# The head of an int4 SwiGLU + S4 kernel: token blocks transposed operand by operand, sums in place, buffers moved, all engines reordered until unit 2

## What is computed

```
xn = layernorm(x)
out = x + s4(xn) + ffn(xn)

# ffn: int4 weights, groups of 64 with scale and zero
Wg, Wu, Wd = dequantize(gate_Wq, ...), dequantize(up_Wq, ...), dequantize(down_Wq, ...)
h = silu(xn @ Wg.T) * (xn @ Wu.T)      # 2048 x 2752
ffn = h @ Wd.T                         # 2048 x 1024

# s4: a kernel of 1024 taps from 64 complex states (Cauchy sums at the roots of unity, inverse FFT),
# then a causal convolution of each row with it, plus D * xn
```

## Time and profile before

| | us |
|---|---|
| median of 3 runs | 1380.62 |
| lowest, highest | 1374.71, 1381.23 |
| the profiled execution | 1377.99 |
| its span in the trace | 1376.2 |

### The profile page before, as it was taken

How to read it: one execution, slowest core, us unless ns; L and a number is a source line. 1 busy time by engine, 2 the same in 40 slices (tenths; PEclk the granted TensorE clock), 3 DMA queues, 4 the chain that set the end, 5 groups by cost and what they waited for, 6 DMA issues and landing times.

```text
span 1376.2 us, 16940 instructions
## 1 busy us (share of the span) xinstructions
PE 1313.8 (95%) x6302; PEld 625.4 (45%) x6302; DVE 917.0 (67%) x1008; ACT 461.8 (34%) x815; POOL 665.4 (48%) x484
## 2 busy tenths in 40 slices
PE   3688999999999999999999999899999999999998
PEld 2454444444444444444444444344444444444444
DVE  7965798989989889997797977434434423241432
ACT  5744444555455454544454544310000000000000
POOL 6862776878878787875686877520000000000000
PEclk8799999999999999999999999999999999999999
DMA  9111554454646454544455455999373344336331
GB/s 315 34 47 39 156 159 153 141 181 146 187 131 187 138 179 126 171 152 123 151 153 163 127 157 161 366 395 324 102 235 123 100 156 166 115 100 222 100 100 61
DMA packets 165168, 218.08 MB, mean 158 GB/s; under 512 B 42205, under 2 KB 122719, under 8 KB 163167
## 3 DMA queue, kind: packets, MB, share of 16 engines
q1 hardware_dynamic: 163646, 200.69, 46.7%
q10 hardware_dynamic: 1440, 16.32, 2.9%
HBM read 139.64 MB, written 77.34 MB: 158 GB/s over the span
## 4 chain that ended last, share of the span: by engine, by line
PE 76%; DVE 5%; issue 1%; ACT 1%; POOL 1%; DMA 0%; SPq 0%; ACTq 0%; DVEq 0%
PE px L1382 24%; PE px L1469 17%; PE pz L1382 11%; PE pz L1469 8%; PE py L1382 6%; PE pv L1496 6%; PE py L1469 4%; DVE wf L1554 1%; DVE wf L1551 1%; DVE wf L1555 0%; DMA w_d<-ds 0%; POOL ds L703 0%; DVE hf L1682 0%; POOL hs L713 0%; DVE hf L1685 0%
## 5 line engine op out<-in xcount | busy, mean ns | idle before, releaser
L1382 PE MATMUL px<-xo,wo 128*128 128x512 f16 x2016 | 467.1, 385 | 13.3 <-ACT u L1006 9.5
L1382 PEld LDWEIGHTS px<-xo,wo 128*128 128x128 f16 x2016 | 199.4, 99 | 256.7 <-issue 19.4
L694 POOL TENSOR_TENSOR wo<-wf,wo 128x512 f16<-128x512 f32 x147 | 233.7, 1600 | 69.1 <-ACT wo L952 69.1
L713 POOL TENSOR_TENSOR hs<-hf,hs 128x512 f16<-128x512 f32 x154 | 204.3, 1332 | 99.5 <-ACT hs L987 97.2
L1469 PE MATMUL px<-wd,hr 128*128 128x512 f16 x1056 | 232.3, 379 | 0.0
L1382 PE MATMUL pz<-xo,wo 128*128 128x512 f16 x1008 | 231.3, 379 | 0.1
L1469 PEld LDWEIGHTS px<-wd,hr 128*128 128x128 f16 x1056 | 102.2, 98 | 118.8
L1382 PEld LDWEIGHTS pz<-xo,wo 128*128 128x128 f16 x1008 | 98.6, 98 | 118.6 <-issue 0.8
L952 ACT ACTIVATE wo<-wf 128x512 f16<-128x512 f32 x147 | 91.5, 623 | 89.0 <-DVE wf L1555 81.2
L1554 DVE TENSOR_TENSOR wf<-wf,sz 128x1024 f32<-128x1024 int32 x63 | 118.4, 1879 | 2.2
L1469 PE MATMUL pz<-wd,hr 128*128 128x512 f16 x528 | 116.6, 379 | 0.0
(11 more groups left out here) (230 smaller groups left out, 1387.4 us busy)
## 6 DMA issues: line engine op xcount, KB each, us to landing
h_d<-hs SPq DMA_DIRECT2D x154, 256.0 KB, 2.4
hr<-h_d SPq DMA_DIRECT2D x56, 704.0 KB, 4.3
w_d<-ds SPq DMA_DIRECT2D x73, 256.0 KB, 2.0
wd<-w_d ACTq DMA_DIRECT2D x4, 2816.0 KB, 15.5
sz<-in_sz_gate SPq DMA_DIRECT2D x21, 512.0 KB, 5.1
sz<-in_sz_up SPq DMA_DIRECT2D x21, 512.0 KB, 4.8
sz<-in_sz_down SPq DMA_DIRECT2D x20, 512.0 KB, 5.1
xc_d<-xo SPq DMA_DIRECT2D x8, 1024.0 KB, 7.5
```

The source lines that it names most:

```text
L694: pool.tensor_tensor(w_dest(t, j, 1), w_place_of(j), w_dest(t, j, 0), ALU.subtract).then_inc(wlo_done, 1)
L713: pool.tensor_tensor(hs[:, j, :, 1, :], h_place_of(p, j), hs[:, j, :, 0, :], ALU.subtract)\
L1382: done = pe.matmul(bank[:, :], wo[t % 2][:, j, wp, k * P:(k + 1) * P], xo[p][:, j, xp, k, :], start=(j in (0, 3) and k == 0 and wp == 0 an ...
```

## The change

- **Order of blocks.** The 56 blocks follow a written list BLOCKS that goes by operand over four groups: A11 of groups 0 to 3 stand at places 0, 1, 6 and 10, and so on. Unit 0's product of an operand waits for its own four low parts: 11 for A11, 17 for S1, 23 for S2, 14 for A12, 22 for S3, 27 for S4, 28 for A22.
- **PE.** 15 blocks, the first product, 8 blocks, S1 and so on, by a new list BESIDE that now also spans unit 2: 30 blocks stand before the end of unit 0, 4 inside unit 1, 15 between units 1 and 2, 7 inside unit 2.
- **DVE, ACT, POOL.** Statistics, normalisation and reciprocals of groups 4 to 7 move behind unit 0's first work; the sums are taken in another order; all hand-written orders until unit 2 change.
- **Buffers.** S1 and S2 of a group go to a buffer of four groups per sum (`sums`), shared by both halves; S3 is written over A21 as before, S4 now over A12, so it waits until A12 is transposed. Groups 4 to 7 sit at other places. From this come new waits: `x_high` of groups 4 to 7 waits for all blocks of half 0, for S3 also for all four S1 blocks, for S4 also for all four S2 blocks and for the last of the four S4 sums; `down_nibble` and `down_words` of the first slab wait for group 7's blocks.
- **S4 branch.** The DFT matmuls, the transpose and the matmul move from units 29, 31, 33 to 30, 32, 34, and the DVE pieces behind them from 30, 32, 34 to 31, 33, 35. `roots` stays at 26 to 28.

The amount of work is the same: 56 blocks, the same statistics, sums and products; one small matmul more (the one that opens `py` in units 0 to 2 is also made for unit 3).

```diff
+BLOCKS = [(0, A11), (1, A11), (0, S2), (1, S3), (0, S1), (0, A12), (2, A11), (0, S3), (1, S1), (1, A12), (3, A11),
...
+BESIDE = [15, 23, 24, 24, 24, 30, 30, 30, 30, 30, 32, 32, 33, 34, 49, 50, 53, 56, 56, 56, 56, 56]
...
         def x_sum(q, j):
-            if i == 1:
+            if j == S3:
                 return x_tiles(q)[:, 1, 0:SB]
+            if j == S4:
+                return x_tiles(q)[:, 0, SB:2 * SB]
+            return sums[:, 0 if j == S1 else 1, q % 4, :]
...
             def x_sum_of(q, j):
+                if q >= 4 and j in (S1, S2):
+                    pool.wait_ge(xt_done, BLOCK[q - 4, j] + 1)
+                if q >= 4 and j == S2:
+                    pool.wait_ge(xsum_done, sum_place_of(q - 4, S4) + 1)
+                if j == S4:
+                    pool.wait_ge(xt_done, BLOCK[q, A12] + 1)
...
             def x_high(n):
-                q, j = n // 7, X_ORDER[n % 7]
-                act.wait_ge(xt_done, n + 1)
+                q, j = BLOCKS[n]
+
+                act.wait_ge(xt_done, max([n + 1] + [transposed(k) for k in range(4) if q >= 4] +
+                                         [BLOCK[k, S1] + 1 for k in range(4, 8) if q >= 4 and j == S3] +
+                                         [BLOCK[k, S2] + 1 for k in range(4, 8) if q >= 4 and j == S4] +
+                                         [transposed(4) for k in range(1) if q >= 4 and j == A22]))
+                if q >= 4 and j == S4:
+                    act.wait_ge(xsum_done, max(sum_place_of(k, S4) for k in range(4, 8)) + 1)
...
             def down_nibble(g, h):
+                if g + h == 0:
+                    act.wait_ge(xt_done, transposed(7))
...
             def products(n, t, p, j):
-                if n == 0:
-                    pe.wait_ge(xlo_done, max(22 + X_POS[j], head_banks_free(("x0", "y0", "z0"), 28)))
+                if n in (0, 2):
+                    pe.wait_ge(xlo_done, max(BLOCK[q, j] for q in range(4 * p, 4 * p + 4)) + 1)
...
-                if n == 29:
+                if n == 30:
                     pe.wait_ge(roots_done, 1)
...
-            for b in range(28):
-                x_transposes(b)
-            for n in range(2):
+            blocks = 0
+            for n in range(3):
                 for i, j in enumerate(TURN):
-                    products(n, n, 0, j)
-                    for b in range(*BESIDE[7 * n + i]):
+                    for b in range(blocks, BESIDE[7 * n + i]):
                         x_transposes(b)
+                    blocks = BESIDE[7 * n + i]
+                    products(n, n % 2, n // 2, j)
```

More of the change, by code:

```diff
@@ L1120, in _ @@
-            snap_u2(1)
-            for b in range(42, 44):
-                x_high(b)
-            snap_u3(1)
-            x_high(44)
-            silu_first(1)
-            x_high(45)
-            silu_second(1)
-            for b in range(46, 56):
+            normalize(5)
+            snap_s5(1)
+            h_high(0, 0, A11)
+            snap_u2(1)
+            x_high(30)
+            normalize(6)
+            x_high(31)
+            silu_first(1)
+            w_high(1, T4)
+            normalize(7)
@@ L1129, in _ @@
+            x_high(32)
+            snap_u3(1)
+            x_high(33)
+            h_high(0, 0, A12)
+            silu_second(1)
+            for b in range(34, 49):
+                x_high(b)
+            snap_s1(2)
+            x_high(49)
+            snap_s5(2)
+            x_high(50)
+            h_high(0, 0, A22)
+            for b in range(51, 53):
+                x_high(b)
+            h_high(0, 0, S3)
+            snap_u2(2)
+            for b in range(53, 56):
                 x_high(b)
@@ L1568, in down_words @@
             def down_words(g, h):
+                if g + h == 0:
+                    dve.wait_ge(xt_done, transposed(7))
                 if g >= 1:
```

316 lines of the change are left out of this document (143 added, 173 removed).

## The result

| | before | changed |
|---|---|---|
| time, median (lowest to highest) | 1377.66 us (1374.16 to 1381.23, 4 runs) | 1360.31 us (1357.89 to 1363.57, 4 runs) |
| profiled execution | 1377.99 us, span 1376.2 | 1358.25 us, span 1356.5 |
| mean granted clock | 0.978 | 0.992 |

The ratio of the times is 0.9875, with a 95% interval of 0.9834 to 0.9917: 1.25% faster. A later set, with the changed kernel run once more, gave 1358.97 us (1358.08 to 1372.55, 6 runs) beside 1379.69 (1372.60 to 1380.10, 11 runs) for before, ratio 0.9886 (0.9849 to 0.9923); the ratio isn't the quotient of the two medians, which is 0.9850. The forecast was 1359.6 us in a range of 1351 to 1370, so the time is right to a microsecond. How far its terms are right is another question.

The account below looks back on a forecast made before the run. DVE was taken to bound the kernel up to 58 us, PE from 202 us. Head 17.5 plus S4 branch 3.5 gives 21.0 us: 1357.0 for the profiled execution, 1359.6 for the median, range 1351 to 1370.

Parts of the forecast that it names:

- Part 1: Head: DVE runs 11 fewer low parts and 4 fewer statistics, 18.6 to 19.8 us; first product at about 38.2.
- Part 2: Unit 0: PE waits 2.5 us before S1, S4 starts at 63, unit 0 ends at 68.3 against 85.98 before.
- Part 3: Unit 1 and second-half blocks: unit 1 runs 68.3 to 88.7, 15 blocks take 9.0 us, unit 2 starts at 97.9.
- the walk: Hand trace of the four engines' lists at profiled durations, from the first product to unit 4; gain 19.8 us.
- The prediction's test: Units 0 and 1: wrong if PE idles above 12 us between 38 and 100 us, or clock there is under 0.9.
- Part 4: Units 2 and 3: old `snap_u2` wait goes, seven blocks come, unit 3 waits some 1.4 us; unit 4 at 139.2.
- The 2.3 us taken off the walk: Head: allowance for slab contention and a slowed S1 product, cutting the gain from 19.8 to 17.5 us.
- the 3.8: Two slabs' four DVE steps: most that contention with POOL could cost, of which some 1 us hits PE.
- From there DVE, ACT, POOL follow as before: From unit 4 on: same lists follow PE's products, unit 4's 4.01 us wait stays, the gain is kept.
- Part 5: S4 branch, units 29 and 30: `roots` wait goes, `snap_u2(29)` is late next; gain 3.5 us, bounds 1.7 and 4.2.
- Held by order: Rival: three or four ACT or POOL crossings come late, half the head's gain goes, some 1368 us; chance 0.20.
- The slow clock in units 0 and 1: Rival: PE stays sparse, each of 14 products slowed, 24 to 35 us lost, 1389 in the middle; chance 0.04.

Follow-up runs that it names:

- stats_first: Changed kernel with DVE's statistics of groups 4 to 7 back between the low parts ahead of the first product; 1371.24 us, one run.
- product_late: Changed kernel with unit 0's first product behind 23 blocks instead of 15 and `snap_s1(0)` later on ACT; 1356.06 us, one run.
- Both unit 3 experiments: Changed kernel with DVE's T1 sum of slab 2 ahead of `h_s3(0, 1)` (1357.00 us), or ACT's `snap_u2(3)` ahead of two weight parts (1355.70 us).
- numerators_later: Changed kernel with `snap_u2(3)` and slab `down(0, 1)` taken earlier, plus DVE's convolution scalar work and its chain one unit later; 1354.78 us, one run.
- t1_sooner: Changed kernel with ACT's high parts of T1 and T3 behind three instead of eight high parts of blocks 15 to 22; 1359.28 us, one run.

## Why the prediction was right, and where it was not

- **Part 1, first product: right in size, wrong in meaning.** 38.2 was forecast, 39.77 measured; DVE's list without a gap, 11 low parts and 4 statistics shorter, is what moved it. `stats_first` put 12.0 to 13.2 us of this back, the first product came 10.0 later, and nothing of that was made up. That the product came 1.6 us later than forecast cost 0.9 us at unit 1. But the prediction spoke as if the first product's start were what is gained. `product_late` shows that it is not: 6.1 us later there, 1.0 earlier in unit 1.
- **Part 2: right.** The wait before S1 is 2.53 us (2.5 forecast), S4 starts at 63.78 (63), unit 1 at 69.19 (68.3). The 0.9 us are the first product's delay, part of it caught up.
- **Part 3: right.** Unit 2 at 98.86 (97.9), 29.67 us after unit 1 (29.6 by the walk). The prediction's test is met: PE is idle 4.4 us from 38 to 100, and the clock there is 0.97.
- **Part 4: two terms right, one mis-sized.** Unit 2's old wait went and the blocks came: 21.66 us, 21.7 by the walk. Unit 3's wait was forecast at 1.4 us and is 2.99, and a slowed product (4.05 for 2.75) follows it; unit 3 takes 22.67 us, 19.6 by the walk. The slab `up(2)` ends at 128.5, as forecast (129). The step that failed is the one behind it, from the slab to `snap_u2(3)`: it left out that DVE is held 2.23 us by POOL's `h_low` ahead of `h_s3`, which stands in front of the T1 sum. Both unit 3 experiments bring the unit back to the walk. Unit 4's wait stayed (3.85 us for 4.01), as the prediction said.
- **The 2.3 us taken off the walk** were meant for contention and a slowed product in unit 0. In the first trace S1's product ran at full speed (in five others it took 4.14 to 4.44 us). Of the four slab steps three took 1.22 us while POOL was idle, and the one at 58.75 took 2.17 beside a sum: 1.0 us of the 3.8, which left a wait of 0.26 ahead of S4. The loss in unit 3 was not in the haircut: the start of unit 4 gained 15.8 us, for 17.5 forecast. By its size the haircut was too small, by its place wrong.
- **"From there DVE, ACT, POOL follow as before": nearly.** From unit 4 to unit 7 it is 61.59 us for 61.46. A wait of 1.51 us at 197.00 is larger than before (0.28), and unit 4's wait and product are 1.1 us shorter (3.85 and 4.26 for 4.01 and 5.22); DVE's list sets this stretch in both kernels, which the prediction had not added up. DVE's rise from 66.41 to 72.76 us of 86 is no more work: the list of units 4 to 6 starts 15.8 us sooner, so more of it lies in the stretch. From unit 7 to 29 another 1.1 us are lost, all in unit 14 (19.25 us for 18.16, with waits of 0.33 and 0.47); the prediction had none. `numerators_later` has none of these waits; why unit 14 has them wasn't sought.
- **Part 5: mechanism right, mis-sized.** The order of events is as foretold, with `snap_u2(29)` as what is late next, after 1.87 us (2.1 forecast). The price of a slowed product behind this wait, 0 to 2.5 us of which some 0.7 was taken, is zero in each trace that has this wait. So the step gave 4.4 us net, and not 3.5, over its bound of 4.2. From unit 31 on another 0.8 us went (710.9 for 711.7 to the end). Two traces of one kernel differ by as much: the second trace of the changed kernel takes 711.7 there.
- **The sum**: 14.6 + 4.4 + 0.8 gives, but for rounding, the 19.7 us of the span, for 21.0 forecast. The errors were -2.9 in the head and +1.7 behind it, and that they cancel in part is luck. In the profiled executions this is 1358.25 us for 1357.0; the median of before was lower in this set than in the one that the forecast started from, 1377.66 for 1380.62, which hid part of the miss: the difference of the medians is 17.35 us. That the median came to within a microsecond is luck to that extent.
- **The rivals.** Held by order (1368): unit 3 is one case of it, not three or four. The slow clock in units 0 and 1 (1389): PE did not stay sparse; the clock from 58 to 116 us is 1.00. Only the first product ran a little slow, at 3.46 us, while in `product_late` it took 2.75: there the slow clock fell on blocks. The sentence of the Trainium skill (TensorE: Matmul & The Clock Gate, "What's actually happening") on the throttled default state agrees with the traces in direction (granted clock 0.60 from 29 to 39 us, where PE waits between blocks, 1.00 from 58 to 116), but doesn't tell which products behind a wait are slowed. The rule of the Trainium skill (SBUF — State Buffer, "Who interferes with whom"), by which all 3.8 us would be lost (1362.4), is not excluded by the time, but the loss is not where it would put it: from the first product to unit 2 the changed kernel takes 59.09 us, and the walk without any contention 59.7. What it asks for, a busy POOL, was there for one of the four slab steps, and that one took 2.17 us. `t1_sooner` shows the rule at work too, with 1.44 and 1.53 for 0.68 and 0.69 us.

## What to carry to other kernels

Look for the point from which the array is busy without a gap, and count what each feeding engine must have done by then: only work moved from before that point to behind it is gained, and the start of the first product is a poor measure of it. Behind that point take the feeding engine's busy time over several units, not over one wait; when that engine has no idle time left, a wait that is reordered away comes back in part, one or two units later, and moving work off the crowded stretch helps (here 8.2 us of small work by one unit, 2.3 us in unit 6). A step with slack elsewhere, such as a side branch whose matmuls stand in the main queue, costs its whole wait and is moved a unit later almost for free.
